# Scan of a hybrid layer stack: GpSimd works on two scan steps at a time, the residual goes to TensorE and its read-out to ScalarE

## The chip, the core and the metric

One core of a Trainium2 chip runs the whole kernel. The metric is the device time of one execution in microseconds; the kernel before took 3098.16 us (median of three runs, 3097.73 to 3105.76). Engines are called PE (TensorE), DVE (VectorE), ACT (ScalarE), POOL (GpSimd) and SP (SyncE, which here only issues DMAs).

## What is computed

Four layers over x of shape 8 x 512 x 512 (batch, position, channel): a selective state-space scan, a mixture of experts, attention, the same mixture of experts. The change touches only the first. Cut to what matters:

```python
xz = einsum('bld,kd->blk', xn, W_x)              # xn = layernorm(x)
dt = softplus(dt_raw @ W_dt.T + b_dt)
d_a = exp(dt[..., None] * a)                     # 16 states per channel
dbx = dt[..., None] * b_ssm[:, :, None, :] * xn[..., None]
h   = d_a[t] * h + dbx[t]                        # over t
y_t = einsum('bdn,bn->bd', h, c_ssm[t])
x1  = x + y + xn * D_param
```

## The kernel before

The scan works with channels on the 128 partitions and 512 positions along the row. A step k is one block of 128 channels (HC = 4 blocks c) with one group g of NG = 2 of the 16 states; STEPS = 32 steps make a batch, NSTEP = 256 steps the whole scan. Steps k and k + 1 (k even) are the two blocks of one half of the channels for the same group, so both use the same rows of B and C (`bc`, one DMA of 1 MB for every two steps, NBC = 3 buffers).

One step runs through four engines:

- POOL `feed` (line 1796) writes dt·x·B for both states into a buffer of `hb` (128x1024; HB = 5 buffers of one step).
- ACT `decay` (line 1654) writes exp(a·dt) for the two states into PSUM banks 2, 3, 4 in turn, so it can be at most one and a half steps ahead of the scan.
- DVE `scan` (lines 1292 and 1296) waits for the feed and the decays, runs two scans along the row, and multiplies the second state by C. 
- POOL `weigh_c` (line 1802) multiplies the first state by C (128x512), once its scan is done.
- PE `y_sum` (line 970) adds both states, transposed, into a PSUM bank of y, one bank for even and one for odd blocks; at g = 0 it first puts in xn·D (line 965). The feed of step k waits for the sum of step k - HB.

After the eighth group of a block, DVE `x1` (line 1302) adds the y bank onto the row buffer `xin` (which holds x), two steps behind the scan (X1_BEHIND = 2). The next sum into that bank waits for it.

Every engine executes its instructions in the order of one written plan (`scan_plan`). It is a list of items; each engine takes from it the items that it has a function for. The tables at lines 55 to 65 say at which of the 32 steps of a batch the other work stands: the preparation of the next batch (layernorm, projections, softplus with `dt_sum` on DVE at line 1283 and `dtx` on POOL at line 1787), the router of the previous batch (`route1` with line 1361, `masks` with line 1381, `pick` with lines 1389 and 1392) and its shared expert (PE lines 998, 1019, 1033, 1039; ACT line 1673; DVE lines 1315 and 1330). The feed of step k + 2 stands ahead of the scan of step k (AHEAD = 2).

```python
plan += [("scan", k), ("weigh_c", k)]
```

After the scan come a short routing chain, the experts, attention and the second mixture; they are not touched but for one small ring (OUT) that holds rows of the shared expert.

Of the kernel before, what the change touches and what calls it, by code (L numbers as in the profile page):

```python
# [15 lines left out]
P = 128  # L16
# [25 lines left out]
NG = 2  # L42
# [4 lines left out]
HB = 5  # L47
NBC = 3
AHEAD = 2
# [14 lines left out]
FIRST_DT, FIRST_SOFT = (0, 0), (("soft_exp", 3), ("soft_ln", 4), ("dt_sum", 5), ("dtx", 6))  # L64
X1_BEHIND = 2
# [20 lines left out]
ABREAST, OUT = (1, 2), (3, 4)  # L86
# [236 lines left out]
def scan_plan():  # L323
# [12 lines left out]
    for k in range(NSTEP + X1_BEHIND):  # L336
        if k + AHEAD < NSTEP:
            plan += [("feed", k + AHEAD)]
        if k < NSTEP:
            b, c, g = step_of(k)  # L340
            plan += [("scan", k), ("weigh_c", k)]
            if c % 2 == 0 and k // 2 + NBC - 1 < NSTEP // 2 and k > 0:
                plan += [("bc_in", k // 2 + NBC - 1)]
# [6 lines left out]
        if 0 < k <= NSTEP:  # L350
            plan += [("sum", k - 1)]
# [7 lines left out]
    plan += own[:OUT[0]]  # L359
    for more in chain:  # L360
# [4 lines left out]
        for kind in TAKEN_BESIDE.get(name, ()):  # L365
            plan += [i for i in pending if i[0] == kind]
            pending = [i for i in pending if i[0] != kind]
        if name == "pick4":
            plan += own[OUT[0]:]
# [204 lines left out]
class Program:  # L574
# [76 lines left out]
    def list_memory(self, sb, m):  # L651
# [3 lines left out]
        f["own"], f["twice"] = sb.cut([1]), sb.cut([1])  # L655
# [41 lines left out]
    def scan_memory(self, sb):  # L697
# [11 lines left out]
        self.hb = [sb.cut([NG, SEQ]) for _ in range(HB)]  # L709
# [187 lines left out]

    def da_bank(self, k, n):
# [12 lines left out]
def tensor_engine(p, eng):  # L911
# [44 lines left out]
    def y_sum(k):  # L956
        b, c, g = step_of(k)
        s, w, each = b % 2, p.hb[k % HB], b * HC + c
# [8 lines left out]
        for n, by in enumerate(("pool", "dve")):  # L967
            PE.wait_ge(p.weighted[by], k)
# [248 lines left out]
def vector_engine(p, eng):  # L1217
# [67 lines left out]
    def scan(k):  # L1285
        b, c, g = step_of(k)
        h = p.hb[k % HB]
        banks = [bank[p.da_bank(k, n)] for n in range(NG)]
        V.wait_ge(p.fed, k)
# [888 lines left out]
```

## Time and profile before

| | before |
|---|---|
| median of 3 runs | 3098.16 us |
| lowest, highest | 3097.73, 3105.76 us |
| profiled execution, its time | 3104.51 us |
| its span in the profile | 3102.7 us |
| busy PE, DVE, ACT, POOL | 2788.7, 1774.2, 1292.9, 1526.5 us |
| scan stage | from about 37 to 1060 us of the span |

The span is cut into 40 slices of 77.6 us on the page; slices 2 to 13 are the scan, where DVE and POOL are both at nine tenths or more. Times below are microseconds from the start of the span. "Idle before" is the time that the engine stood still just before the instruction, with what ended that wait. Groups of instructions give the total busy time and the mean of one. Durations of consecutive instructions overlap a little, so the distance from start to start is the better measure where an engine never stops.

### The profile page before, as it was taken

The page shows a single profiled execution, that of the slowest core. Times are in us where ns is not written, and L with a number is a line of the kernel's source. Part 1 is how long each engine was busy: PE and PEld are TensorE (multiplying, and loading weights), DVE is VectorE, ACT ScalarE, POOL GpSimd, SP SyncE. Part 2 cuts the span into 40 slices and gives each one's busy share as a digit, 9 for nine tenths or more (in the row PEclk, how much of TensorE's full clock was granted, in tenths as well). Part 3 has the DMA queues.
Part 4 walks back from the last instruction along what each step waited for, and adds up shares of the span by engine and source line. Part 5 has one row for each costly group of instructions (what it writes and reads, how often), then busy time and mean ns, then how long its engine had stood idle before and what let it go on. Part 6 is the DMA issues. An engine that isn't in the chain of part 4 may idle for free.

```text
span 3102.7 us, 38070 instructions
## 1 busy us (share of the span) xinstructions
PE 2788.7 (90%) x13772; PEld 1502.6 (48%) x13772; DVE 1774.2 (57%) x3723; ACT 1292.9 (42%) x2681; POOL 1526.5 (49%) x943
## 2 busy tenths in 40 slices
PE   4668989988998889988868999999899999999998
PEld 2455555655555534433335555555545454444443
DVE  5899999999999742222246666665433434222222
ACT  4557577675765401110126666767612220111111
POOL 5999999999999512211135555554300000111212
PEclk7669999999998989999989999999999999999999
DMA  5444545545545579999930000002034223999997
GB/s 183 147 165 154 192 167 165 195 164 176 174 161 179 184 259 359 347 341 337 331 107 1 28 28 28 28 29 74 28 115 171 97 85 87 307 345 345 342 353 213
DMA packets 198957, 557.80 MB, mean 180 GB/s; under 512 B 24880, under 2 KB 26800, under 8 KB 198256
## 3 DMA queue, kind: packets, MB, share of 16 engines
q1 hardware_dynamic: 180624, 513.27, 48.0%
q0 software_dynamic: 17088, 40.90, 5.8%
q8 instruction: 109, 1.79, 0.2%
q10 hardware_dynamic: 1056, 1.18, 0.1%
q14 instruction: 80, 0.66, 0.1%
HBM read 479.50 MB, written 75.79 MB: 179 GB/s over the span
## 4 chain that ended last, share of the span: by engine, by line
PE 42%; DMA 8%; DVE 4%; SPq 4%; ACT 3%; POOL 2%; issue 2%; POOLq 0%; DVEq 0%; ACTq 0%
PE bank L1099 7%; PE bank L998 5%; PE bank L1019 5%; PE bank L1146 4%; DMA arena<-in_w_up 4%; PE bank L1203 3%; PE bank L1033 3%; DMA out<-arena 3%; PE bank L1125 3%; PE bank L1180 3%; PE bank L1168 2%; SPq L2037 2%; ACT arena L1717 2%; POOL arena L1892 2%; PE bank L1192 1%
## 5 line engine op out<-in xcount | busy, mean ns | idle before, releaser
L1796 POOL TENSOR_TENSOR arena<-arena 128x1024 f32<-128x1024 f32 x256 | 605.3, 2365 | 7.1 <-PE bank L970 4.0
L1654 ACT ACTIVATE bank<-arena 128x512 f32<-128x512 f32 x512 | 346.3, 689 | 316.8 <-DVE arena L1292 198.6
L1892 POOL TENSOR_TENSOR arena<-arena 128x2048 f32<-128x2048 f32 (+3 forms) x128 | 296.6, 2320 | 285.8 <-DVE arena L1522 285.8
L970 PE MATMUL bank<-arena 128*128 128x128 f32 x2048 | 308.5, 304 | 137.8 <-POOL arena L1802 137.6
L970 PEld LDWEIGHTS bank<-arena 128*128 128x128 f32 x2048 | 262.4, 157 | 223.9 <-POOL arena L1802 176.8
L1717 ACT ACTIVATE arena<-arena 128x256 f32<-128x256 f32 (+3 forms) x512 | 285.9, 561 | 189.6 <-DVE arena L1513 159.2
L1802 POOL TENSOR_TENSOR arena<-arena 128x512 f32<-128x512 f32 x256 | 333.3, 1302 | 19.8 <-DVE arena L1292 19.8
L1099 PE MATMUL bank<-arena 128*64 128x352 f32 x2048 | 333.5, 481 | 0.0
L1292 DVE TENSOR_TENSOR_SCAN arena<-bank,arena 128x512 f32<-128x512 f32 x256 | 310.9, 1214 | 25.5 <-POOL arena L1796 19.4
L1292 DVE TENSOR_TENSOR_SCAN bank<-bank,arena 128x512 f32<-128x512 f32 x256 | 308.5, 1205 | 0.0
L1019 PE MATMUL bank<-arena 128*128 128x512 f32 x640 | 288.3, 593 | 9.1 <-ACT arena L1673 9.1
L998 PE MATMUL bank<-arena 128*128 128x512 f32 x640 | 291.3, 598 | 4.3 <-DVE arena L1330 2.4
L1033 PE MATMUL bank<-arena 128*128 128x512 f32 x640 | 286.2, 598 | 0.0
L1860 POOL DMA_INDIRECT arena<-scratch_xn,arena x64 | 68.7, 1074 | 370.1 <-DVE arena L1481 139.9
L1454 DVE TENSOR_TENSOR arena<-arena,bank 128x352 f32<-128x352 f32 x64 | 33.4, 521 | 371.0 <-PE bank L1099 325.4
L1513 DVE CUSTOM_DVE_ANT_0 arena<-bank,arena 128x256 f32<-128x256 f32 (+3 forms) x512 | 220.5, 486 | 39.6 <-PE bank L1168 34.1
L1691 ACT ACTIVATE arena<-bank 128x352 f32<-128x352 f32 x64 | 29.6, 463 | 480.2 <-PE bank L1099 423.7
L1099 PEld LDWEIGHTS bank<-arena 128*64 128x64 f32 x2048 | 146.6, 142 | 152.1 <-issue 147.5
L1019 PEld LDWEIGHTS bank<-arena 128*128 128x128 f32 x640 | 120.4, 190 | 161.6 <-issue 145.9
L1296 DVE TENSOR_TENSOR arena<-bank,arena 128x512 f32<-128x512 f32 x256 | 177.1, 692 | 18.1 <-DVE bank L1292 0.5
L1033 PEld LDWEIGHTS bank<-arena 128*128 128x128 f32 x640 | 118.9, 192 | 137.9 <-issue 137.8
L998 PEld LDWEIGHTS bank<-arena 128*128 128x128 f32 x640 | 117.6, 192 | 132.4 <-issue 126.7
(139 smaller groups left out, 4130.9 us busy)
## 6 DMA issues: line engine op xcount, KB each, us to landing
arena<-scratch_bc SPq DMA_DIRECT2D x128, 1024.0 KB, 5.4
arena<-in_w_gate SPq DMA_DIRECT2D x128, 704.0 KB
arena<-in_w_up SPq DMA_DIRECT2D x128, 704.0 KB
arena<-in_w_down SPq DMA_DIRECT2D x128, 512.0 KB
arena<-in_w_down SPq DMA_DIRECT2D x128, 192.0 KB
scratch_x<-arena SPq DMA_DIRECT2D x16, 1024.0 KB, 4.6
scratch_xn<-arena SPq DMA_DIRECT2D x15, 1024.0 KB, 4.2
arena<-scratch_x SPq DMA_DIRECT2D x44, 256.0 KB, 6.0
```

The source lines that it names most:

```text
L970: i = nc.tensor.matmul(y[:, t * P:(t + 1) * P], w[:, n, t * P:(t + 1) * P], p.ident, is_transpose=True, start=False, stop=g == GROUPS - 1 ...
L998: i = nc.tensor.matmul(out[:, :], f["swg"][:, c, j * P:(j + 1) * P], xnT[:, c, :], start=c == 0, stop=c == HC - 1)
L1019: i = nc.tensor.matmul(out[:, :], f["swu"][:, c, j * P:(j + 1) * P], xnT[:, c, :], start=c == 0, stop=c == HC - 1)
L1033: nc.tensor.matmul(out[:, :], f["shT"][:, j, t * P:(t + 1) * P], f["swd"][:, j, :], start=j == 0, stop=False)
L1099: i = nc.tensor.matmul(bank[1 + w][mine, 0:INTER], f["xeT"][k % 2][:, c, mine], f["ring"][(2 * k + half) % nw][w][:, c, :], start=c == 0, ...
L1292: nc.vector.tensor_tensor_scan(out=banks[n][:, :] if n else h[:, n, :], data0=banks[n][:, :], data1=h[:, n, :], initial=0.0, op0=ALU.mult, ...
L1513: nc.vector.tensor_tensor_reduce(out=p.sc[i % NSC][:, 0:width], in0=bank[c][:, 0:width], in1=p.amask[:, SEQ - width:], scale=-SCALE, scala ...
L1654: nc.scalar.activation(bank[p.da_bank(k, n)][:, :], block_of(p.dt, b, c), ACT.Exp, scale=p.alog[:, c, state:state + 1]).then_inc(*p.decaye ...
L1717: nc.scalar.activation(p.pr[n % 2][:, c, OFFSET[t]:OFFSET[t] + width], p.sc[i % NSC][:, 0:width], ACT.Exp, scale=-1.0, bias=p.nb[:, k % 2, ...
L1796: nc.gpsimd.tensor_tensor(out=p.hb[k % HB], in0=over(block_of(p.dtx, b, c), 1, NG), in1=p.bc[k // 2 % NBC][:, 0], op=ALU.mult).then_inc(*p ...
L1802: nc.gpsimd.tensor_tensor(out=h, in0=h, in1=p.bc[k // 2 % NBC][:, 1, 0, :], op=ALU.mult).then_inc(*p.weighted["pool"].up(k))
L1892: nc.gpsimd.tensor_tensor(out=own, in0=own, in1=over(p.rden[:, k % 2, :], 2, width), op=ALU.mult).then_inc(*p.divided.up(k))
```

## The change

- `feed` and `weigh_c` on POOL are made for two steps at once: 128x2048 and 128x1024 elements in one instruction. `hb` is now HB = 3 buffers of two steps (six steps in place of five). AHEAD = 1 counts pairs. The feed of pair n + 1 stands ahead of scan 2n; the weighing of pair n stands behind scan 2n + 1 and waits for that step's first scan.
- `sum` of both steps of a pair stands together, behind the work of the next even step.
- x is put into the y bank by PE (four 128x128 products with the identity at g = 0, per block), and `x1` becomes a plain copy from PSUM to `xin` on ACT, three steps behind.
- The waits on `fed` and on the pool's `weighted` count pairs, in `dt_out`, in the DMA of `bc` and in the sums.
- The tables of steps are new. OUT of the first mixture is 2 in place of 3, and the fetches of the last rows are spread out.

```diff
-HB = 5
+HB = 3
-AHEAD = 2
+AHEAD = 1
-PREPARE = (("x_in", 4), ("stats_a", 7), ("stats", 8), ("rstd", 8), ("apply", 11))
-TURN_S, DTR, BC, DT = (13, 13, 14, 14), 16, 15, (21, 21, 22, 25)
-SOFT = (("soft_exp", (24, 28)), ("soft_ln", (26, 29)), ("dt_sum", (27, 30)), ("dtx", (28, 31)))
-FRONT = (("stats_a", 1), ("stats", 1), ("rstd", 1), ("apply", 3), ("xn_out", 3), ("gate", 7), ("logit", 9), ("route_max", 10), ("route_exp", 12), ("route1", 13), ("masks", 15))
-TURN_F, FOLD = (5, 5, 5, 6), 18
-PICK_AT = (22, 23, 24, 27, 33, 35, 37, 41)
-GATES, UPS = (23, 26, 29, 30, 32, 35), (23, 26, 29, 30, 33, 35)
-DOWNS = (40, 41, 43, 51)
+PREPARE = (("x_in", 5), ("stats_a", 9), ("stats", 9), ("rstd", 9), ("apply", 11))
+TURN_S, DTR, BC, DT = (12, 12, 13, 13), 14, 20, (16, 17, 20, 20)
+SOFT = (("soft_exp", (20, 24)), ("soft_ln", (24, 25)), ("dt_sum", (28, 30)), ("dtx", (28, 30)))
+FRONT = (("stats_a", 2), ("stats", 2), ("rstd", 2), ("apply", 4), ("xn_out", 4), ("gate", 11), ("logit", 12), ("route_max", 14), ("route_exp", 16), ("route1", 21), ("masks", 22))
+TURN_F, FOLD = (6, 6, 7, 7), 25
+PICK_AT = (27, 30, 31, 31, 40, 42, 43, 48)
+GATES, UPS = (24, 26, 28, 30, 33, 36), (24, 27, 29, 30, 33, 36)
+DOWNS = (40, 41, 49, 54)
-X1_BEHIND = 2
+X1_BEHIND = 3
-ABREAST, OUT = (1, 2), (3, 4)
+ABREAST, OUT = (1, 2), (2, 4)
...
-        if k + AHEAD < NSTEP:
-            plan += [("feed", k + AHEAD)]
+        if k % 2 == 0 and k // 2 + AHEAD < NSTEP // 2:
+            plan += [("feed", k // 2 + AHEAD)]
-            plan += [("scan", k), ("weigh_c", k)]
+            plan += [("scan", k)] + [("weigh_c", k // 2)] * (k % 2)
...
-        if 0 < k <= NSTEP:
-            plan += [("sum", k - 1)]
+        if 0 < k <= NSTEP and k % 2 == 0:
+            plan += [("sum", k - 2), ("sum", k - 1)]
...
+            for t in range(QT):
+                nc.tensor.matmul(y[:, t * P:(t + 1) * P], p.ident, p.xin[s][:, t, c * P:(c + 1) * P],
+                                 start=False, stop=False, skip_group_check=True)
...
-    def x1(b, c):
-        x = p.xin[b % 2][:, :, c * P:(c + 1) * P]
-        V.wait_ge(p.y_summed, step_at(b, c, GROUPS - 1))
-        nc.vector.tensor_tensor(out=x, in0=x,
...
+    def x1(b, c):
+        A.wait_ge(p.y_summed, step_at(b, c, GROUPS - 1))
+        nc.scalar.copy(p.xin[b % 2][:, :, c * P:(c + 1) * P], bank[Y_BANKS[c % 2]][:, :].rearrange(
+            "p (t d) -> p t d", t=QT)).then_inc(*p.x1_added.up(b, c))
...
+    def feed(n):
+        b, c, g = step_of(2 * n)
         G.wait_ge(p.dtx_ready, b, c // 2)
+        G.wait_ge(p.bc_in[n % NBC], n)
+        if n >= HB:
+            G.wait_ge(p.y_summed, 2 * (n - HB) + 1)
+        nc.gpsimd.tensor_tensor(out=p.hb[n % HB], in0=over(half_of(p.dtx, b, c // 2), 2, NG),
+                                in1=over(p.bc[n % NBC][:, 0], 1, 2), op=ALU.mult).then_inc(*p.fed.up(n))
+
+    def weigh_c(n):
+        h = p.hb[n % HB][:, :, 0, :]
+        G.wait_ge(p.scanned, 2 * n + 1, 0)
+        nc.gpsimd.tensor_tensor(out=h, in0=h, in1=over(p.bc[n % NBC][:, 1, 0, :], 1, 2), op=ALU.mult).then_inc(
+            *p.weighted["pool"].up(n))
```

## Rows read from the trace of the kernel before

**Rows 1.** Busy time by stretch: PE, PEld, DVE, ACT, POOL, then clock, DMA share, GB/s.
```profile
480.00:620.00 140.00, 128.44 (x602) 77.79 (x600) 134.83 (x170) 95.92 (x138) 136.88 (x83) 0.98 0.54 175
620.00:760.00 140.00, 123.94 (x535) 72.46 (x533) 137.03 (x176) 90.62 (x129) 130.12 (x79) 0.94 0.52 169
```

**Rows 2.** Waits from 100 to 1150 us: who waited for whom, total, times, longest.
```profile
POOL arena L1802 <- DVE arena L1292: 19.8, 9, 2.3
POOL arena L1796 <- PE bank L970: 4.0, 3, 2.5
DVE arena L1292 <- POOL arena L1796: 6.8, 17, 0.5
DVE arena L1292 <- ACT bank L1654: 5.3, 5, 1.8
```

**Rows 3.** Timeline of a stretch with little beside the steps: start, duration, engine.
```profile
489.67 2.36 POOL L1796 TENSOR_TENSOR arena<-arena 128x1024 f32<-128x1024 f32 x1
490.42 0.97 PEld L965 LDWEIGHTS bank<-arena 128*128 128x128 f32 x8
491.99 1.28 POOL L1802 TENSOR_TENSOR arena<-arena 128x512 f32<-128x512 f32 x1
493.21 2.38 POOL L1796 TENSOR_TENSOR arena<-arena 128x1024 f32<-128x1024 f32 x1
...
496.47 1.21 DVE L1292 TENSOR_TENSOR_SCAN arena<-bank,arena 128x512 f32<-128x512 f32 x1
...
499.44 1.21 DVE L1292 TENSOR_TENSOR_SCAN arena<-bank,arena 128x512 f32<-128x512 f32 x1
```

**Rows 4.** Groups of POOL instructions by shape, whole span.
```profile
L1892 POOL TENSOR_TENSOR arena<-arena 128x2048 f32<-128x2048 f32 x32 | 115.2, 3601 | 113.9 <-DVE arena L1522 113.9
L1892 POOL TENSOR_TENSOR arena<-arena 128x1024 f32<-128x1024 f32 x32 | 60.6, 1893 | 39.1 <-DVE arena L1522 39.1
L1787 POOL TENSOR_TENSOR arena<-arena 128x1024 f32<-128x1024 f32 x16 | 37.8, 2362 | 24.3 <-DVE arena L1283 24.3
L1777 POOL TENSOR_TENSOR arena<-arena 128x4 f32<-128x4 f32 x32 | 33.2, 1038 | 2.7
```

**Rows 5.** Groups of DVE instructions by shape, 80 to 1045 us.
```profile
L1283 DVE TENSOR_TENSOR arena<-arena 128x1024 f32<-128x1024 f32 x14 | 49.5, 3538 | 0.0
L1242 DVE BATCH_NORM_STATS2 arena<-arena 128x6 f32<-128x512 f32 x52 | 32.6, 679 | 0.1
L1361 DVE TENSOR_TENSOR arena<-arena 128x256 f32<-128x256 f32 x7 | 8.8, 1252 | 0.2
L1381 DVE TENSOR_SCALAR arena<-arena 128x256 f32<-128x256 f32 x7 | 8.6, 1227 | 0.2
```

**Rows 6.** Timeline around `dt_sum` (L1283), alone at 33.60 and beside POOL.
```profile
33.60 1.22 DVE L1283 TENSOR_TENSOR arena<-arena 128x1024 f32<-128x1024 f32 x1 [20.21 <-ACT arena L1637]
...
143.41 8.67 DVE L1283 TENSOR_TENSOR arena<-arena 128x1024 f32<-128x1024 f32 x1
...
526.85 5.25 DVE L1283 TENSOR_TENSOR arena<-arena 128x1024 f32<-128x1024 f32 x1
...
533.31 1.27 POOL L1802 TENSOR_TENSOR arena<-arena 128x512 f32<-128x512 f32 x1 [2.29 <-DVE arena L1292]
...
541.69 2.13 DVE L1283 TENSOR_TENSOR arena<-arena 128x1024 f32<-128x1024 f32 x1
...
913.93 2.44 DVE L1283 TENSOR_TENSOR arena<-arena 128x1024 f32<-128x1024 f32 x1
```

**Rows 7.** Timeline at the first feeds and behind the last scan.
```profile
37.33 4.64 POOL L1796 TENSOR_TENSOR arena<-arena 128x1024 f32<-128x1024 f32 x2
...
1059.46 0.69 DVE L1302 TENSOR_TENSOR arena<-arena,bank 128x512 f32<-128x512 f32 x1 [8.00 <-PE bank L970]
```

**Rows 8.** DMA issues: size and median time to landing.
```profile
arena<-scratch_bc SPq DMA_DIRECT2D x128, 1024.0 KB, 5.4
```

**Rows 9.** One group of the page: a shared-expert product is eight matmul records.
```profile
L1019 PE MATMUL bank<-arena 128*128 128x512 f32 x640 | 288.3, 593 | 9.1 <-ACT arena L1673 9.1
```

More of the change, by code:

```diff
@@ L359, in scan_plan @@
     plan += own[:OUT[0]]
+    own = own[OUT[0]:]
     for more in chain:
@@ L365, in scan_plan @@
         for kind in TAKEN_BESIDE.get(name, ()):
-            plan += [i for i in pending if i[0] == kind]
+            taken = [i for i in pending if i[0] == kind]
             pending = [i for i in pending if i[0] != kind]
-        if name == "pick4":
-            plan += own[OUT[0]:]
+            plan += taken
+            if kind == "so":
+                plan += own[:len(taken)]
+                own = own[len(taken):]
         for _ in range(MADE_BESIDE.get(name, 0)):
@@ L654, in list_memory @@
         f["wts"], f["key"], f["row"], f["gap"] = (sb.cut([NPAIR]) for _ in range(4))
-        f["own"], f["twice"] = sb.cut([1]), sb.cut([1])
+        columns = sb.cut([2])
+        f["own"], f["twice"] = columns[:, 0:1], columns[:, 1:2]
         f["tok"] = sb.cut([CAP])
@@ L708, in scan_memory @@
         self.bc = [sb.cut([2, NG, SEQ]) for _ in range(NBC)]
-        self.hb = [sb.cut([NG, SEQ]) for _ in range(HB)]
+        self.hb = [sb.cut([2, NG, SEQ]) for _ in range(HB)]
     def row_memory(self, sb):
@@ L896, in ring_with, with states @@
         return next(r for r in self.rings if key in r.index)
+    def states(self, k):
+        return self.hb[k // 2 % HB][:, k % 2]
     def da_bank(self, k, n):
@@ L957, in y_sum @@
         b, c, g = step_of(k)
-        s, w, each = b % 2, p.hb[k % HB], b * HC + c
+        s, w, each = b % 2, p.states(k), b * HC + c
         y = bank[Y_BANKS[c % 2]]
@@ L966, in y_sum @@
                                  start=t == 0, stop=False, skip_group_check=True)
-        for n, by in enumerate(("pool", "dve")):
-            PE.wait_ge(p.weighted[by], k)
+            if b > 0:
+                PE.wait_ge(p.x_in[s], b)
+            for t in range(QT):
+                if b == 0:
+                    PE.wait_ge(p.x_first[t], 0)
+                nc.tensor.matmul(y[:, t * P:(t + 1) * P], p.ident, p.xin[s][:, t, c * P:(c + 1) * P],
+                                 start=False, stop=False, skip_group_check=True)
+        for n, (by, made) in enumerate((("pool", k // 2), ("dve", k))):
+            PE.wait_ge(p.weighted[by], made)
             for t in range(QT):
@@ L1543, in vector_engine @@
     work = {"constants": constants, "barrier": barrier, "stats": stats, "stats_a": stats_a, "apply": apply, "decay_w": decay_w,
-            "dt_sum": dt_sum, "scan": scan, "x1": x1, "hid": hidden, "so": shared_out,
+            "dt_sum": dt_sum, "scan": scan, "hid": hidden, "so": shared_out,
             "route_max": route_max, "route1": route1, "masks": masks, "folded": folded, "pick": pick, "merge": merge, "lists": lists,
@@ L1623, in dt_out @@
         if before >= 0:
-            A.wait_ge(p.fed, (before + 1) * STEPS // 2 - 1)
+            A.wait_ge(p.fed, (before + 1) * STEPS // 4 - 1)
         nc.scalar.activation(block_of(p.dtx, b, c), out[:, :], ACT.Abs, bias=p.par[:, c, 0:1])
@@ L1743, in scalar_engine @@
             "dt_out": dt_out, "soft_exp": soft_exp, "soft_ln": soft_ln, "decay_w": decay_w, "scan": decay,
-            "logit": logit, "silu": silu, "route_exp": route_exp, "up": expert_gate, "flip": flipped, "scale": scale,
+            "x1": x1, "logit": logit, "silu": silu, "route_exp": route_exp, "up": expert_gate, "flip": flipped, "scale": scale,
             "mask": exped, "pcopy": probs_flipped, "weighed": weighed}
@@ L1788, in dtx @@
                                 op=ALU.mult).then_inc(*p.dtx_ready.up(b, h))
-    def feed(k):
-        b, c, g = step_of(k)
+    def feed(n):
+        b, c, g = step_of(2 * n)
         G.wait_ge(p.dtx_ready, b, c // 2)
-        G.wait_ge(p.bc_in[k // 2 % NBC], k // 2)
-        if k >= HB:
-            G.wait_ge(p.y_summed, k - HB)
-        nc.gpsimd.tensor_tensor(out=p.hb[k % HB], in0=over(block_of(p.dtx, b, c), 1, NG), in1=p.bc[k // 2 % NBC][:, 0],
-                                op=ALU.mult).then_inc(*p.fed.up(k))
-    def weigh_c(k):
-        h = p.hb[k % HB][:, 0, :]
-        G.wait_ge(p.scanned, k, 0)
-        nc.gpsimd.tensor_tensor(out=h, in0=h, in1=p.bc[k // 2 % NBC][:, 1, 0, :], op=ALU.mult).then_inc(
-            *p.weighted["pool"].up(k))
+        G.wait_ge(p.bc_in[n % NBC], n)
[8 more added lines that the diff above has]
+            *p.weighted["pool"].up(n))
     def route_w(m):
```

12 lines of the change are left out of this document (5 added, 7 removed).

## The prediction

> **What bounds the kernel now.** I read the page's slices first: the scan fills the first third of the span, and DVE and POOL are both full in it. By stretch, POOL is busy 136.88 of 140 us and DVE 134.83, PE 128.44 [rows 1]. No engine is plainly the bound; three are near it. So the next view is who waits for whom: from 100 to 1150 us POOL waits 19.8 us for scans, DVE 6.8 us for feeds and 5.3 us for decays, POOL 4.0 us for sums [rows 2]. DVE and POOL take turns, and what counts is the sum of work on each and how much either may run ahead.
>
> **POOL now.** Where nothing stands beside, feed starts at 489.67, weighing at 491.99, the next feed at 493.21: 2.32 + 1.22 = 3.54 us a step [rows 3], 113.3 a batch. Add two `dtx` (2.33 each, from [rows 4] less the overlap) and two `rstd` chains of short instructions, the longest 1.04 [rows 4], some 1.9 each with their gaps: 121.8. A batch really takes 128.4 us: `dt_sum` of batch 0 starts at 143.41, that of batch 6 at 913.93 [rows 6].
>
> **DVE now.** Two steps back to back are 2.97 us apart (496.47 to 499.44) [rows 3]; with gaps I take 3.0, so 96 a batch. `dt_sum` is 6.8 a batch (49.5 over about 7.3 batches), `x1` 2.8, the rest of the beside-work about 20.7; 126.3 in all. Of that, `dt_sum` alone needs 1.22 and takes 3.54 on the mean beside POOL [rows 5, 6].
>
> **What the change does to each.**
> 1. *Two steps in one POOL instruction.* The fixed part of an instruction is, by start-to-start distances, 2 x 1.22 - 2.32 = 0.12 us; by durations, the attention's rows give 1893 x 2 - 3601 = 185 ns [rows 4]. Two instructions less a pair: 0.24 to 0.37 us, and I take 0.28. A pair goes from 7.08 to 6.80 (feed 4.49, weighing 2.31), a batch from 113.3 to 108.8: 4.5 us of POOL a batch, 36 in all (31 to 47). That broadcasting over the outer dimension is free is shown: `dtx` without it takes 2362 ns [rows 4], the feed with it 2.36 to 2.38 [rows 3]. If the longer form saved nothing, the 36 is lost (bound from the other side: zero).
> 2. *x1 off DVE.* 32 times 0.69 [rows 7], less the overlap: 19.5 us of DVE. The ACT copy costs about 0.6 and waits for `y_summed`, with the decays of the following steps behind it. ACT is busy 96 of 140 us [rows 1]; by the walk below it gets to the copy about when the sums are done and has 4 us before DVE needs the next decay. Cost taken: nothing; without that air it is the PE lag, up to 3.6 us a time.
> 3. *Residual on PE.* Four products like those of line 965, whose weight loads take 0.97 us for a block [rows 3]: 31 us in all, 3.9 a batch, in the pair of g = 0. PE's need is then some 116 us of a batch of 125. It is hidden if PE runs at 2.4 GHz and a sum never lags by more than the 6.8 us until the feed that waits for it; the shared expert's worst chunk before a sum (three products of 288.3 / 80 = 3.6 us [rows 9] at steps 29 and 30) falls where `dt_sum` holds the others up anyway.
> 4. *bc DMA.* Its buffer is freed 6.8 us before its feed (7.1 before) and it lands in 5.4 [rows 8]. Hidden; margin 1.3 us.
> 5. *Less room between the engines.* Before, scan k could start from the end of its feed to 1.2 us before its weighing is due, a window of 6.1 us. Now the feed of a pair ends 2.4 us before the next feed starts, and the odd step's first scan must be done 4.5 us after that: a window of 2.5 us. Each burst of DVE beyond it idles POOL.
> 6. *The shared port.* `dt_sum` reads two SBUF operands. Alone it takes 1.22 us; at 541.69 it waited for the running POOL instruction, took 2.13, and stretched the next weighing to 2.25; at 526.85 it was passed over by further POOL instructions until POOL itself stood still for 2.29 us; at 143.41 that cost 8.67 [rows 6]. 4 of 14 were passed over. After the change `dtx` stands right behind the same feed and waits for `dt_sum`, so nothing can pass it; it waits for the rest of one feed, which is now up to 4.5 us long. The same holds for lines 1361 and 1381 (1.25 and 1.23 us, some 0.33 when alone) [rows 5].
>
> The Trainium skill (SBUF — State Buffer, the section on its two separate sides) says that of a GpSimd operation and such a DVE one the second comer blocks until the first has finished. By that rule nobody waits for more than the rest of one POOL instruction, and the third rival below could not happen: its chance would go to the forecast. The trace agrees for 10 of 14 `dt_sum` and disagrees for 4, so that rival keeps a chance.
>
> **The walk.** I went through a batch pair by pair with these numbers: POOL feed(n+1) 4.49, then weighing(n) 2.31, not before the odd step's first scan; DVE 3.0 a step plus what the new tables put beside it (statistics 3.0 at steps 2 and 9, four rows of 0.68 [rows 5] and their aggregate; a pick 1.3; a shared-expert item 0.6); port operations at the end of the running feed. The weighing of pairs 0 to 15 ends, in a batch with picks at 8, 10, 11 and 16, at 6.8, 15.5, 22.3, 29.1, 35.9, 46.1, 53.7, 60.5, 67.6, 74.4, 81.2, 90, 96.8, 103.6, 113.9, 124.2. The two long ones at the end are `dt_sum` and `dtx`: 20.6 us for two pairs, 2.3 more than POOL's own work. A batch with picks at 27 to 31 takes 121.7, but leaves DVE 4 us late into the next. Two batches are 249.9, so 125.0 each. The walk has neither ACT nor PE in it; before, waits for those were 5.3 + 4.0 us over 7.5 batches [rows 2], so I add 1.3: 126.3.
>
> **Sum.** Batches 1 to 6: 6 x (128.4 - 126.3) = 13 us. Batch 0, paced by POOL, 4. Batch 7, without preparation, 4. The first scan waits for a feed of two steps (4.5 in place of 2.3 [rows 7]): -2. At the end x1 waits 8.00 us for PE's backlog of shared-expert work [rows 7]; in the new order the last sums stand behind less of it but the weighing is 1.1 longer: +2. Together 21, rounded to 20. The profiled execution took 3104.5, so 3084.5 on its scale; the median is 6.3 us lower: 3078.
>
> **The rivals.**
> - *All of POOL's saving arrives* (3060, chance 0.12). If DVE is never late, 36 us of POOL come through and the passed-over turns of `dt_sum` go too: 3098 - 38. For it: x1 is off DVE. Against: DVE's own sum, 96 + 19 + 2.2 + port waits of 8, is about 125 a batch.
> - *The lost room eats it* (3090 to 3107, likeliest 3097, chance 0.25). Stalls of 2 to 3 us a batch beyond the walk (a PE chunk at a lower clock: the stretch 620 to 760 has 0.94 granted [rows 1]; ACT behind a table load and the x1 copy; or the long form saving nothing) make six batches worth 126.3 + 2.5 = 128.8. For it: three engines busy 92% or more of a stretch [rows 1]. Against: the waits for ACT and PE were small before.
> - *Slower: the router's operations are passed over* (3117, chance 0.18). Line 1361 at step 21 has a weighing and the next feed queued on POOL ahead of any wait for DVE. If it is passed over by both, it waits 6.8 us in place of 1.5, scan 22 starts 4.8 later and POOL stands for as long. The same can happen to line 1381. At 4.8 us each it takes 4 of the 14 to undo the forecast's 20, and 6 of 14 make it slower by 9; 8 of 14 give 3078 + 39 = 3117. For it: 4 of 14 `dt_sum` were. Against: lines 1361 and 1381 average 1.25, so they seldom were.
>
> **How the numbers follow.** Forecast 3078 (3069 to 3088), chance 0.45. A difference under about 0.3% (9.3 us) can't be told from none. Faster 0.45 + 0.12 = 0.57, same 0.25, slower 0.18. The range reaches from the first rival, 3058, over the second to the edge of the third, 3110.
>
> **What would show it.** Feeds of 4.5 us and weighings of 2.36 us, 128 each; both start-to-start distances adding to 6.8 where nothing stands beside. `dt_sum` never above about 5.5 us. `dt_sum` starts 126 us apart from batch to batch. The waits of the weighing for the scan rise above 19.8 us in total (the lost room), to perhaps 60. DVE's waits for ACT and POOL's for PE stay under 20 us. The prediction is wrong if the feed of 2048 takes over 4.7 us, if POOL waits for PE or DMA by tens of us, or if line 1361 or 1381 takes over 5 us in most batches.

## The result, and the profile after

| | before | after |
|---|---|---|
| median, measured side by side (5 runs after) | 3102.38 us | 3118.29 us (3115.13 to 3123.92) |
| ratio after / before | | 1.0056 [1.0039, 1.0072] |
| profiled execution: its time, its span | 3104.51, 3102.7 us | 3123.92, 3122.1 us |
| first scan starts, last scan starts | 39.70, 1048.93 us | 40.87, 1070.64 us |
| experts start (DVE's first product of gate and up, line 1454, after 1462) | 1131.08 us | 1150.19 us |
| from there to the end of the span | 1971.6 us | 1971.9 us |

The change makes the kernel slower by 0.56%, some 17 us. The forecast was 3078, its range ended at 3110. The last two rows say where the time stands: the experts begin 19.1 us later, what follows takes as long as before, and the spans differ by 19.4. The whole loss is in the scan stage.

First what went as forecast, on POOL. Timeline of after, the same kind of stretch as [rows 3]:

```profile
497.06 2.36 POOL L1815 TENSOR_TENSOR arena<-arena 128x1024 f32<-128x1024 f32 x1
499.37 4.53 POOL L1809 TENSOR_TENSOR arena<-arena 128x2048 f32<-128x2048 f32 x1
503.86 2.37 POOL L1815 TENSOR_TENSOR arena<-arena 128x1024 f32<-128x1024 f32 x1
```

Weighing to feed 2.31, feed to weighing 4.49: 6.80 us for a pair, which was 7.08. Groups of POOL by shape, 40 to 1080 us:

```profile
L1809 POOL TENSOR_TENSOR arena<-arena 128x2048 f32<-128x2048 f32 x128 | 580.1, 4532 | 24.8 <-DMA arena<-scratch_bc 12.7 <-PE bank L985 11.5
L1815 POOL TENSOR_TENSOR arena<-arena 128x1024 f32<-128x1024 f32 x128 | 303.8, 2373 | 50.8 <-DVE arena L1307 48.7 <-DMA arena<-scratch_bc 2.0
```

The means of 4532 and 2373 ns are the forecast's. What is new stands behind the second bar: POOL now stands still in front of both, 24.8 and 50.8 us in all. Who waited for whom in after, 80 to 1100 us (total, times, longest), to be read against [rows 2]:

```profile
POOL arena L1815 <- DVE arena L1307: 48.7, 32, 4.2
DVE arena L1307 <- ACT bank L1662: 29.5, 30, 2.0
POOL arena L1800 <- DVE arena L1298: 16.7, 14, 1.4
DVE arena L1307 <- POOL arena L1809: 12.4, 14, 3.1
POOL arena L1809 <- PE bank L985: 11.5, 11, 2.6
POOL arena L1809 <- DMA arena<-scratch_bc: 9.2, 6, 2.8
```

POOL's wait for scans went from 19.8 to 48.7 us, DVE's for decays from 5.3 to 29.5, POOL's for sums from 4.0 to 11.5. So POOL did less and waited longer, and DVE is what it waited for. Why DVE is late is in its groups of after, 80 to 1080 us:

```profile
L1298 DVE TENSOR_TENSOR arena<-arena 128x1024 f32<-128x1024 f32 x15 | 41.5, 2766 | 0.0
L1360 DVE TENSOR_SCALAR arena<-arena 128x4 f32<-128x4 f32 x7 | 17.0, 2428 | 0.2
L1369 DVE TENSOR_TENSOR arena<-arena 128x256 f32<-128x256 f32 x7 | 12.8, 1827 | 0.2
L1389 DVE TENSOR_SCALAR arena<-arena 128x256 f32<-128x256 f32 x7 | 11.8, 1686 | 0.2
```

Lines 1369 and 1389 are 1361 and 1381 of before [rows 5]; 1360 is line 1352 of before, which negates four numbers per partition and took 3.0 us in its seven batches. In the forecast it doesn't occur. That line in before, duration min/median/max in ns:

```profile
L1352 DVE TENSOR_SCALAR arena<-arena x7: 170/342/891, 208.1 to 976.7; 128x4 f32<-128x4 f32 x7
```

and the three in after:

```profile
L1360 DVE TENSOR_SCALAR arena<-arena x7: 1669/2150/3275, 224.1 to 1010.3; 128x4 f32<-128x4 f32 x7
L1369 DVE TENSOR_TENSOR arena<-arena x7: 760/2042/2222, 247.4 to 1034.3; 128x256 f32<-128x256 f32 x7
L1389 DVE TENSOR_SCALAR arena<-arena x7: 293/2133/2326, 252.9 to 1040.5; 128x256 f32<-128x256 f32 x7
```

An operation that needs 0.17 us took 1.67 to 3.28 in each of seven batches. One of them, with the feed that ran beside it:

```profile
349.96 4.52 POOL L1809 TENSOR_TENSOR arena<-arena 128x2048 f32<-128x2048 f32 x1
351.23 3.27 DVE L1360 TENSOR_SCALAR arena<-arena 128x4 f32<-128x4 f32 x1
```

The feed ends at 354.48 and the negation at 354.50; in all seven batches the negation ends 0.03 us after the feed does. So it waits for the rest of the running POOL instruction, and that rest can now be twice as long. Where the line falls within POOL's cycle counts as well: in the runs below it takes 9.9 us with single steps and the new tables, and 16.1 us with pairs and the old ones.

DVE's account from the first scan to the last, after less before: line 1352/1360 +14.0 us (3.0 to 17.0), line 1361/1369 +4.0, line 1381/1389 +3.2, waits for decays +25.6 (5.6 to 31.2), waits for feeds +2.1 (14.5 to 16.6), `dt_sum` -9.2 (50.7 to 41.5, 15 each), `x1` -21.3 (30 of 678 ns and 0.9 of waits). That makes +18.4 of the 20.5 us by which this time rose (1009.23 to 1029.77).

The waits for decays crowd: 22.7 of the 31.2 us stand at steps 25 to 27 of a batch, where before has 4.4. ACT's timeline in after, one batch, some lines between left out:

```profile
387.76 1.28 ACT L1645 ACT_TABLE_LOAD   x1
389.06 1.06 ACT L1645 ACTIVATE arena<-arena 128x1024 f32<-128x1024 f32 x1
390.13 1.28 ACT L1640 ACT_TABLE_LOAD   x1
391.43 1.06 ACT L1640 ACTIVATE arena<-arena 128x1024 f32<-128x1024 f32 x1
392.39 1.28 ACT L1662 ACTIVATE bank<-arena 128x512 f32<-128x512 f32 x2
393.69 1.28 ACT L1645 ACT_TABLE_LOAD   x1
394.99 1.06 ACT L1645 ACTIVATE arena<-arena 128x1024 f32<-128x1024 f32 x1
396.06 1.28 ACT L1662 ACT_TABLE_LOAD   x1
397.36 1.30 ACT L1662 ACTIVATE bank<-arena 128x512 f32<-128x512 f32 x2
398.68 1.28 ACT L1686 ACT_TABLE_LOAD   x1
...
400.59 1.28 ACT L1662 ACT_TABLE_LOAD   x1
```

and DVE beside it:

```profile
393.10 1.22 DVE L1307 TENSOR_TENSOR_SCAN arena<-bank,arena 128x512 f32<-128x512 f32 x1 [0.59 <-ACT bank L1662]
...
398.15 1.22 DVE L1307 TENSOR_TENSOR_SCAN arena<-bank,arena 128x512 f32<-128x512 f32 x1 [1.99 <-ACT bank L1662]
...
402.61 1.22 DVE L1307 TENSOR_TENSOR_SCAN arena<-bank,arena 128x512 f32<-128x512 f32 x1 [0.72 <-ACT bank L1662]
```

Softplus is an exp (line 1640) and a log (1645) for each half of the channels, silu (1686) is the shared expert's, and each of these stands in another table than its neighbour. From 387.76 to 401.87 stand six loads of 1.28 us and only four decays, and so in six batches; in before no six loads in a row have fewer than six decays among them. The number of loads hardly changed (105 before, 100 after, 80 to 1050 us); the new tables of steps put the log of one half, the exp of the other and its log at steps 24, 24 and 25, with two silus right behind. The Trainium skill (ScalarE: Activation LUTs, What ACT_TABLE_LOAD costs) gives 1283 ns for the load and 1380 ns more for a drain. The load agrees; the drain isn't here, since the activation starts 1.30 us after its load did (387.76, 389.06) and the next load starts when that activation ends (389.06 + 1.06, 390.13).

### The profile page after: what moved, and what is told of

Read it like the earlier page. It is cut to its first block, busy times and chain, and to the rows that moved or that the text cites. A ratio compares the mean times of both kernels' runs of the same rounds, so it can differ in the third digit from the quotient of the medians.

```text
span 3122.1 us, 38187 instructions
## 1 busy us (share of the span) xinstructions
PE 2806.8 (90%) x14028; PEld 1533.7 (49%) x14028; DVE 1767.2 (57%) x3691; ACT 1310.1 (42%) x2715; POOL 1485.5 (48%) x687
## 4 chain that ended last, share of the span: by engine, by line
PE 46%; DMA 5%; DVE 4%; SPq 3%; ACT 3%; POOL 2%; issue 1%; POOLq 0%; DVEq 0%; ACTq 0%
PE bank L1114 8%; PE bank L1013 5%; PE bank L1034 5%; PE bank L1048 4%; PE bank L1161 4%; PE bank L1140 4%; DMA arena<-in_w_up 4%; PE bank L1218 3%; PE bank L1195 3%; PE bank L1183 2%; SPq L2050 2%; ACT arena L1730 2%; POOL arena L1905 2%; PE bank L1207 1%; DVE arena L1521 1%
## 5 line engine op out<-in xcount | busy, mean ns | idle before, releaser
L1809 POOL TENSOR_TENSOR arena<-arena 128x2048 f32<-128x2048 f32 x128 | 580.1, 4532 | 24.8 <-DMA arena<-scratch_bc 12.7
L985 PE MATMUL bank<-arena 128*128 128x128 f32 x2048 | 290.3, 301 | 116.6 <-POOL arena L1815 116.0
L1307 DVE TENSOR_TENSOR_SCAN arena<-bank,arena 128x512 f32<-128x512 f32 x256 | 310.7, 1214 | 55.0 <-ACT bank L1662 31.2
L1815 POOL TENSOR_TENSOR arena<-arena 128x1024 f32<-128x1024 f32 x128 | 303.8, 2373 | 50.8 <-DVE arena L1307 48.7
L1013 PE MATMUL bank<-arena 128*128 128x512 f32 x640 | 290.6, 597 | 15.5 <-ACT arena L1686 6.5
```

Source lines behind the costliest of these rows:

```text
L985: i = nc.tensor.matmul(y[:, t * P:(t + 1) * P], w[:, n, t * P:(t + 1) * P], p.ident, is_transpose=True, start=False, stop=g == GROUPS - 1 ...
L1013: i = nc.tensor.matmul(out[:, :], f["swg"][:, c, j * P:(j + 1) * P], xnT[:, c, :], start=c == 0, stop=c == HC - 1)
L1307: nc.vector.tensor_tensor_scan(out=banks[n][:, :] if n else h[:, n, :], data0=banks[n][:, :], data1=h[:, n, :], initial=0.0, op0=ALU.mult, ...
L1809: nc.gpsimd.tensor_tensor(out=p.hb[n % HB], in0=over(half_of(p.dtx, b, c // 2), 2, NG), in1=over(p.bc[n % NBC][:, 0], 1, 2), op=ALU.mult). ...
L1815: nc.gpsimd.tensor_tensor(out=h, in0=h, in1=over(p.bc[n % NBC][:, 1, 0, :], 1, 2), op=ALU.mult).then_inc(*p.weighted["pool"].up(n))
```

## The experiments

All in pairs with the kernel before on the same chip, five rounds each. Two measures stand in the table: the ratio of the times, and the start of the experts (DVE's first product of gate and up) in the one profiled execution (before 1131.08, after 1150.19). From there to the end the 17 profiles took between 1969.4 and 1980.4 us without an order that I can see, so of two profiles a difference under some 8 us in the whole says little; the ratios decide.

| kernel | ratio [95%] | experts start |
|---|---|---|
| after | 1.0056 [1.0039, 1.0072] | 1150.2 |
| move_only | 1.0025 [1.0011, 1.0040] | 1128.8 |
| move_three_behind | 1.0012 [0.9998, 1.0026] | 1126.5 |
| single_steps_new_tables | 1.0124 [1.0101, 1.0148] | 1162.4 |
| pairs_old_tables | 1.0123 [1.0095, 1.0152] | 1167.0 |
| pairs_x1_on_dve | 1.0066 [1.0045, 1.0087] | 1154.3 |
| split_pairs | 1.0146 [1.0129, 1.0164] | 1177.9 |
| more_room | 1.0072 [1.0056, 1.0087] | 1156.8 |
| same_tables_no_room | 1.0068 [1.0055, 1.0080] | 1151.0 |
| no_table_loads | 0.9991 [0.9980, 1.0002] | 1131.0 |
| room_and_no_table_loads | 1.0039 [1.0025, 1.0054] | 1135.8 |
| router_off_port | 0.9983 [0.9967, 1.0000] | 1129.3 |
| router_off_port_soft_joined | 0.9973 [0.9958, 0.9988] | 1118.3 |
| both_causes_removed | 0.9963 [0.9948, 0.9979] | 1120.0 |
| before_no_table_loads | 1.0001 [0.9986, 1.0016] | 1126.5 |
| before_router_off_port | 0.9994 [0.9981, 1.0007] | 1124.0 |

### The parts one by one

**move_only**: the kernel before with the residual on PE and x1 as a copy on ACT, two steps behind.

```diff
 # y_sum, g == 0
+            for t in range(QT):
+                nc.tensor.matmul(y[:, t * P:(t + 1) * P], p.ident, p.xin[s][:, t, c * P:(c + 1) * P],
+                                 start=False, stop=False, skip_group_check=True)
...
-        nc.vector.tensor_tensor(out=x, in0=x, in1=..., op=ALU.add)
+        nc.scalar.copy(p.xin[b % 2][:, :, c * P:(c + 1) * P], ...)
```

> The kernel before with one part of the change alone: the residual goes into the y bank on PE and x1 becomes a copy on ACT, two steps behind the scan; one step per POOL instruction and the tables of before. Theory 1 (the lost room between POOL and DVE is what made the changed kernel slower, the move itself is good): DVE is rid of 32 x 0.62 us = 19.5 us and the time falls by 5 to 15 us against before, to about 3092. Theory 2 (the move is the cost: the copy holds up the decays on ACT, the residual makes sums late on PE): 5 us or more above before, and DVE's wait for decays rises from 5 us towards 29 us. Theory 3 (the new tables are the cost): as theory 1.

**single_steps_new_tables**: the same with the new tables of steps (those of the first batch, FIRST_DT and FIRST_SOFT, with them) and x1 three behind.

```diff
-PREPARE, ..., DOWNS of before;  X1_BEHIND = 2
+PREPARE, ..., DOWNS of after;   X1_BEHIND = 3
```

> All of the change but the pairing: one step per POOL instruction, five single buffers, two steps ahead and the sums step by step as before, with the residual on PE, the copy on ACT and the new tables. Against the changed kernel this adds 128 x 0.28 = 36 us of POOL work and gives the room back. Theory 1 (room): about as fast as before or faster, 3085 to 3105. Theory 2 (the move): about the changed kernel's time, 3118. Theory 3 (the tables, with ACT's softplus and silu work crowded at steps 20 to 28): 3115 or above, since the crowding stays and POOL is slower by 36 us.

**pairs_old_tables**: after, with the tables of before (FIRST_DT and FIRST_SOFT with them).

```diff
-PREPARE, ..., DOWNS of after
+PREPARE, ..., DOWNS of before
```

> The changed kernel with the tables of steps of the kernel before (where the work beside stands); pairs on POOL, residual on PE, copy on ACT three steps behind stay. Theory 1 (room): within 10 us of the changed kernel or slower, since the tables of before are laid out for single steps. Theory 3 (tables): clearly under 3118, 3100 or less, with DVE's wait for decays back near 5 us.

**pairs_x1_on_dve**: after, with x1 back on DVE and without the residual on PE (the reverse of the first diff).

> The changed kernel with x1 back on DVE as an addition, three steps behind, and no residual on PE: pairs and new tables stay. Theory 1 (room): DVE has 19.5 us more and the room stays small, so 5 to 20 us above the changed kernel, about 3130. Theory 2 (the move is the cost): 10 us or more under the changed kernel, with DVE's wait for decays and POOL's for sums well below 29 and 11.5 us.

Measured: 1.0025, 1.0124, 1.0123, 1.0066, that is 8, 38, 38 and 20 us above before, where after is 17 above. None of the three theories comes through: move_only fits the second, single_steps_new_tables the third, pairs_old_tables speaks against the third, and pairs_x1_on_dve, 3 us above after, fits none. What follows is read from the traces.

The move alone doesn't bring the 15 to 20 us that DVE gives up. Waits of move_only, 80 to 1100 us:

```profile
ACT arena L1659 <- PE bank L977: 76.9, 26, 11.3
DVE arena L1299 <- ACT bank L1654: 22.0, 17, 1.9
```

The copy stands in ACT's order ahead of the next decays and waits for the sums 26 times, 77 us in all; DVE's waits for decays go from 5.3 to 22.0, which uses up most of the 20 us of `x1`. In the changed kernel the move gives nothing that can be told from none: 1.0056 with it, 1.0066 without, both intervals 0.003 to 0.004 wide.

The tables belong to the pairs. With the old ones the pairs lose 21 us more (1.0123): the comparison (line 1389) takes 3791 ns on the mean and `dt_sum` 4110, and POOL waits 82.6 us for scans. With the new ones single steps lose 35 us more than with the old (1.0124 against 1.0012 of move_three_behind, below); min/median/max of the router's normalising line there:

```profile
L1361 DVE TENSOR_TENSOR arena<-arena x6: 5011/7549/7672, 246.7 to 911.2; 128x256 f32<-128x256 f32 x6
```

The seventh, in the last batch, took 1.10. A median of 7.5 us for a thing of 0.42 is more than the rest of any one POOL instruction there (2.36 on the mean, 3.34 at most): POOL's next ones went first.

**move_three_behind**: move_only with the copy one step later.

```diff
-X1_BEHIND = 2
+X1_BEHIND = 3
```

> move_only with the copy on ACT three steps behind the scan in place of two. In move_only ACT waited 76.9 us at the copy for the sums, with the decays behind it, and DVE 22 us for decays. If that in-order wait is what took back the 20 us of DVE: ACT's wait at the copy falls under 25, DVE's for decays under 12, the time by 8 to 15 us, to about 3097. If the residual on PE is the cost: no change from 3109.

Measured 1.0012. The copy's waits fall from 76.9 to 16.8 us and DVE's for decays from 22.0 to 9.2, as expected; the time falls by 4 us where 8 to 15 were expected, and each of the two ratios is uncertain by as much. So the waits behind the copy are real, and their price isn't told apart from none. The rest of the move's cost stays open. One lead is that `dt_sum` takes 55.5 and 56.6 us in the two runs where it took 50.7 (15 each). But in both profiles the experts start a little before those of the kernel before, and move_only's first mixture (to the attention's first reciprocal) then takes 489.6 us where it took 484.1, with nothing in the change to explain it.

### What a longer POOL instruction is worth

**split_pairs**: after, each paired operation as two of half the size, the order and the signals as they are.

```diff
+        for i in range(2):
+            x = nc.gpsimd.tensor_tensor(out=p.hb[n % HB][:, i], in0=over(half_of(p.dtx, b, c // 2)[:, i, :], 1, NG),
+                                        in1=p.bc[n % NBC][:, 0], op=ALU.mult)
+        x.then_inc(*p.fed.up(n))
...
```

The weighing is split in the same way.

> The changed kernel with each paired POOL operation issued as two of half the size, back to back, in the same order and with the same signals: only the merging is undone. It costs POOL 0.24 to 0.37 us a pair, 31 to 47 us in all. If POOL's own work sets the pace: 3118 + 30 to 45 = about 3155. If DVE sets it (port waits, late decays): under 15 us more; shorter POOL instructions also shorten each port wait, which can bring it back to 3118 or below.

Measured 1.0146, 28 us slower than after. Groups of DVE in it, 80 to 1080 us, and its wait for feeds, 80 to 1100 us:

```profile
L1298 DVE TENSOR_TENSOR arena<-arena 128x1024 f32<-128x1024 f32 x15 | 31.0, 2070 | 0.0
L1369 DVE TENSOR_TENSOR arena<-arena 128x256 f32<-128x256 f32 x7 | 30.6, 4374 | 0.2
L1360 DVE TENSOR_SCALAR arena<-arena 128x4 f32<-128x4 f32 x7 | 10.9, 1556 | 0.2
...
DVE arena L1307 <- POOL arena L1810: 38.9, 35, 3.4
```

At the port DVE neither wins nor loses: line 1369 rises from 12.8 to 30.6 us (up to 8.1 us for one), line 1360 falls from 17.0 to 10.9, `dt_sum` from 41.5 to 31.0, line 1389 from 11.8 to 10.5, together 83.1 and 83.0. What rises is DVE's wait for feeds, from 12.4 to 38.9 us. POOL is busy 44 us more from the first scan to the last, and 28 of them are paid, near the 30 that I had set for POOL's own work. So the merging is worth 28 us in the changed kernel, and neither POOL nor DVE has time to spare: in this kernel a delay on either is mostly paid.

Long instructions make each wait at the port longer and make it rarer that a DVE operation is passed over. I count an operation as passed over when a whole POOL instruction ran within its recorded time. Of the 36 of `dt_sum` and the three router lines from the first scan to the last these are 0 in after and 4 in split_pairs, 5 in before and 8 in single_steps_new_tables. Pairs don't rule it out: one `dt_sum` each in pairs_old_tables, more_room and room_and_no_table_loads took 8.6, 9.5 and 9.9 us.

### The rival: lost room

**more_room**: after, with four buffers of two steps, four of `bc`, two pairs ahead. Room for it comes from one transposed input of the shared expert in place of two, and two halves of dt in place of three, so the second half's softplus moves to steps 32 to 40 (FIRST_SOFT and MADE_BESIDE are fitted to it).

```diff
-HB = 3
+HB = 4
-NBC = 3
+NBC = 4
-AHEAD = 1
+AHEAD = 2
-TURN_S, DTR, BC, DT = (12, 12, 13, 13), 14, 20, (16, 17, 20, 20)
-SOFT = (("soft_exp", (20, 24)), ("soft_ln", (24, 25)), ("dt_sum", (28, 30)), ("dtx", (28, 30)))
+TURN_S, DTR, BC, DT = (12, 12, 13, 13), 14, 20, (16, 17, 32, 33)
+SOFT = (("soft_exp", (20, 36)), ("soft_ln", (21, 37)), ("dt_sum", (26, 40)), ("dtx", (26, 40)))
```

> The changed kernel with room given back in pairs: four buffers of hb and of bc, and the feed two pairs ahead. The memory comes from one buffer in place of two for the turned rows of the router and two halves in place of three for dt and dtx, for which the second half's softplus moves to steps 32 to 40. Theory 1 (room): POOL's waits for scans and for dt_sum (61 us in the changed kernel) fall under 20 and its waits for the bc DMA (11 us) to nothing; 25 to 35 us under the changed kernel, about 3085 to 3095. Rival 2 (DVE's own sum is the bound: port waits of the router's operations, and decays late on ACT): under 10 us gained, since what DVE loses to the port and to ACT comes back as DVE work, not as room.

**same_tables_no_room** is its control: the same tables and sharing, but HB, NBC and AHEAD as in after.

> The control for more_room: its tables and its smaller rings, but three buffers of hb and bc and the feed one pair ahead, as in the changed kernel. All theories: within 8 us of the changed kernel (3118); what it differs by is the moved softplus, not the room.

Measured 1.0072 and 1.0068. Waits of more_room:

```profile
POOL arena L1815 <- DVE arena L1307: 52.0, 33, 5.3
DVE arena L1307 <- ACT bank L1662: 37.6, 33, 2.6
POOL arena L1809 <- PE bank L985: 17.9, 12, 2.8
...
POOL arena L1809 <- DMA arena<-scratch_bc: 2.0, 2, 1.8
```

and of its control:

```profile
POOL arena L1816 <- DVE arena L1308: 44.0, 28, 4.2
DVE arena L1308 <- ACT bank L1663: 26.9, 26, 2.0
POOL arena L1810 <- PE bank L986: 16.4, 12, 2.7
```

With a pair more of room no scan waits for a feed, which cost 10.3 us in the control, and the DMA of `bc` is in time, and nothing is gained: POOL waits for scans all the same. So with these tables the theory falls. What stands against it is DVE's sum, its waits at the port and for ACT counted in: with more room its waits for decays rise from 26.9 to 37.6 us and `dt_sum` from 43.0 to 49.2. What room is worth with the tables of after this pair can't say.

### The two causes on DVE

**router_off_port**: after, with the router's operations in forms that I expected not to wait for POOL.

```diff
-nc.vector.tensor_reduce(out=f["less"], ..., op=ALU.max)
-nc.vector.tensor_scalar(f["less"], f["less"], -1.0, None, ALU.mult)
+nc.vector.tensor_reduce(out=f["less"], ..., op=ALU.max, negate=True)
-nc.vector.tensor_tensor(out=own, in0=own, in1=over(f["inv"], 2, E), op=ALU.mult)
+for t in range(QT):
+    nc.vector.tensor_scalar(score[:, t, 0:E], score[:, t, 0:E], f["inv"][:, t:t + 1], 0.0, ALU.mult,
+                            ALU.add, accum_out=f["top"][:, t, 7:8])
-nc.vector.tensor_scalar(f["mask"][s], marked[:, :, 0:E], -2.0, None, ALU.is_equal)
+nc.vector.tensor_scalar(f["mask"][s], marked[:, :, 0:E], -2.0, 0.0, ALU.is_equal, ALU.add,
+                        accum_out=f["top"][:, 0, 7:8])
```

> The changed kernel with the three router operations of DVE that wait for POOL in other forms: the maximum is negated by the reduction itself, and the normalising and the comparison are written as scalar operations that also give a sum. In the changed kernel they take 41.6 us in seven batches (20.4 before), alone some 7. Port theory (DVE's own sum is the bound, and longer POOL instructions made these waits longer): they fall to 12 us or less and the time by 15 to 25 us, to about 3098. Late-decay theory alone: under 6 us, since DVE would use the time to wait for ACT.

**before_router_off_port**: the same three edits on the kernel before.

> The kernel before with the same new forms of the three router operations as in router_off_port. There they take 20.4 us in seven batches, so at most some 10 us can go. If the longer POOL instructions are what made them cost 21 us more, this gains 0 to 8 us (3095 to 3102), clearly less than the 18 us of the changed kernel. If it gains 18 here too, the port wait is no part of the difference between the kernels.

Measured 0.9983 and 0.9994. Against after's 1.0056 the edit is worth 0.0073 (give or take 0.0023), 23 us, within the 15 to 25 expected; on the kernel before 0.0006, 2 us, which can't be told from none (its profile has the experts 7 us earlier and the rest 7 us longer). Its lines, min/median/max in ns:

```profile
L1368 DVE TENSOR_SCALAR_CACHE_REDUCE arena<-arena x28: 274/276/281, 246.4 to 1014.4; 128x64 f32<-128x64 f32 x28
...
L1389 DVE TENSOR_SCALAR_CACHE_REDUCE arena<-arena x7: 420/420/421, 252.0 to 1019.4; 128x256 f32<-128x256 f32 x7
```

Beside a full POOL the spread is 1 to 7 ns, and what took 41.6 us in seven batches takes 13.6, the reads of the accumulators included. The Trainium skill (SBUF — State Buffer, Who interferes with whom) says that a scalar operation of DVE can contend with GpSimd, but not the form that also writes out its accumulator, and that a reduction never does. This trace agrees; the reduction takes 408 to 420 ns in it. And POOL's wait for scans falls from 48.7 to 14.9 us: it had been waiting for DVE's port waits.

**no_table_loads**: after, with the log of softplus and the silu of the shared expert beside the scan replaced by a maximum with zero, so no table is loaded there.

```diff
-nc.scalar.activation(soft, soft, ACT.Ln, bias=1.0)
+nc.scalar.activation(soft, soft, ACT.Relu, bias=0.0)
-                             ACT.Silu)
+                             ACT.Relu if m == 0 and q < BATCH - 1 else ACT.Silu)
```

> The changed kernel with ACT's logarithm of the softplus and the silu of the shared expert beside the scan computed as a maximum with zero (this leaves out both functions), so that ACT loads no function tables beside the decays: some 90 loads of 1.28 us less. If decays late on ACT cost the time (28.5 us of DVE waits), those waits go to under 5 and the time falls by 15 to 25 us, to about 3098. If the room alone is the cost, under 8 us.

**before_no_table_loads**: the same edit on the kernel before.

> The kernel before with the same functions left out as in no_table_loads (logarithm of the softplus and silu of the shared expert beside the scan, both a maximum with zero). Late-decay theory: before, DVE waited 5 us for decays, so this gains 0 to 6 us where the changed kernel gained 17. Rival (table loads cost the same in any order of steps and so explain nothing of the difference): 12 us or more.

**room_and_no_table_loads**: more_room with this edit.

> more_room with the functions left out: neither room nor table loads are short. DVE-sum theory: DVE waits for nobody (under 5 us for ACT, under 3 for POOL), the port waits of dt_sum and the router stay at about 90 us, and the time is 3129 less 25 to 35, about 3098. If it comes to 3080 or less, room was short after all, hidden behind the late decays.

Measured 0.9991, 1.0001, 1.0039. In the changed kernel the loads cost 20 us (0.0065, give or take 0.0020), in the kernel before nothing that can be told from none. With more room the late softplus has a new wait: DVE still waits 29.4 us for decays, now 14 times with up to 4.9 us, ACT's copy of x1 waits 31.8 us for sums. So room didn't combine with the cure as I had expected; the tables of more_room cost too much of their own to say what room alone would be worth.

**both_causes_removed**: router_off_port and no_table_loads together.

> The changed kernel with the router operations off the port and with the logarithm of the softplus and the silu beside the scan left out (a maximum with zero). Apart these gained 18 and 17 us. If they are two separate terms of DVE's sum: 30 us or more under the changed kernel, 3080 to 3090, 12 us or more under before. If they overlap (the same idle time counted twice): about 3098.

Measured 0.9963: 29 us below after, where the two gains alone add up to 43, and 11 below before. That is just short of the 30 and 12 that I had set for two separate terms. By the intervals the missing 14 us are uncertain by some 10, so they overlap in part. One group of DVE, 80 to 1080 us, and the waits, 80 to 1100 us:

```profile
L1298 DVE TENSOR_TENSOR arena<-arena 128x1024 f32<-128x1024 f32 x15 | 57.0, 3803 | 0.0
...
DVE arena L1307 <- POOL arena L1809: 26.2, 34, 3.1
...
POOL arena L1809 <- PE bank L985: 21.0, 21, 3.2
...
POOL arena L1809 <- DMA arena<-scratch_bc: 13.2, 6, 3.5
...
POOL arena L1815 <- DVE arena L1307: 9.1, 5, 2.1
```

POOL waits for scans 9.1 us in place of 48.7 and DVE is now the one that waits, for feeds, while POOL waits for sums and for the DMA of `bc`. The terms that were hidden behind DVE come out here. And `dt_sum`, which neither edit touches, takes 57.0 us in place of 41.5: no one takes over 4.8 us, but they meet more of the running feed. These 15.5 us at the port are as much as what is missing; that they are the reason is my reading, and no run tests it. What is left of the change with both causes away is 11 us, half of the 20 forecast.

**router_off_port_soft_joined**: a remedy for each cause that keeps the full computation. The exp of the second half comes a step earlier and both logs stand at step 24.

```diff
-SOFT = (("soft_exp", (20, 24)), ("soft_ln", (24, 25)), ...)
+SOFT = (("soft_exp", (20, 23)), ("soft_ln", (24, 24)), ...)
```

> As router_off_port, and both logarithms of the softplus stand together at step 24 (exponentials at 20 and 23), which saves one pair of table loads a batch and empties step 25. Both causes together: another 3 to 10 us less, about 3090, with DVE's wait for decays at 15 us or less. If late decays don't count: as router_off_port.

Measured 0.9973 [0.9958, 0.9988], 26 us below after and 8 us below before. DVE's waits for decays are 10.1 us, line 1645 loads its table 7 times in place of 14 and line 1640 never. This version beats both kernels. Over router_off_port it gains 3 us, which can't be told from none.

## Why the prediction was wrong

**POOL's instructions (step 1): right.** 4532 and 2373 ns, 6.80 us a pair. The longer form saves what it was to save, and undoing it alone costs 28 us (split_pairs); POOL's own work is busy 125.1 of 140 us where it was 133.5 (means of the two stretches of [rows 1]).

**The walk: the place of the failure.** `dt_sum` of batch 0 and of batch 6 in after:

```profile
148.57 3.71 DVE L1298 TENSOR_TENSOR arena<-arena 128x1024 f32<-128x1024 f32 x1
...
936.18 1.22 DVE L1298 TENSOR_TENSOR arena<-arena 128x1024 f32<-128x1024 f32 x1
```

787.61 / 6 = 131.3 us a batch, where the walk gave 125.0 and the forecast 126.3; before it was 128.4. In six batches that is 30 of the 40 us between the 21 forecast and the 19 lost. Batches 0 and 7, for which the sum has 4 us of gain each, together lost 3.5 (the scans outside these six batches took 238.7 us and take 242.2); that they fail by the same terms isn't shown. Two terms of the walk fail.

- *Step 6, the port.* It named `dt_sum` and lines 1361 and 1381 (which take 0.43 and 0.29 us alone, for the 0.33 given), and missed line 1352, since in the trace of before it is a short thing (0.43 us on the mean). It cost 14 us more, and the three together 21. A short operation's own duration says nothing of what it can wait: that is set by the instruction it meets. For `dt_sum` the step was right: at most 4.34 us, and 41.5 us for 15 in place of 50.7.
- *Step 2, "cost taken: nothing".* I took ACT's spare time from the mean busy share (96 of 140 us) and looked at the x1 copy alone. The tables that the change lays anew put six table loads among four decays. DVE's waits for decays rose by 25.6 us to 31.2, 3.9 a batch, against my sign of under 20 in all; I had 1.3 us a batch for ACT and PE together. The copy as such has its cost where it stands two behind (move_only).

Taking the mean 2.43 us of line 1360 and 29.5 / 7.5 = 3.9 us for decays onto the walk's 125.0 gives 131.3. Such waits overlap, so the sum is no proof by itself. The proof is in the runs: 23 us for the three router lines, 20 for the table loads, 29 for both, and 2 and none on the kernel before.

**Step 3, PE: half right.** POOL's waits for sums rose from 4.0 to 11.5 us, more than hidden, less than a bound. Once DVE is quicker they are 21 (both_causes_removed).

**Step 4, the bc DMA: wrong in size.** Its margin of 1.3 us was of a median landing. POOL's feeds wait 9.2 us for it, up to 2.8 at a time; landings in after have a median of 5.5 us, but reach 9.5 once the scan runs. Hidden in after behind DVE: more_room took the wait away and gained nothing.

**Start and end.** Right. The first scan starts 1.2 us later (forecast 2). From the last scan to the experts it took 82.2 us and takes 79.6: the tail gained 2.6 (forecast 2). The scale was less good: the profiled execution was 6.3 us above the median of three runs, but 2.1 above that of the five measured side by side, by which the forecast would read 3082.

**The rivals.** *The lost room* had the direction of the waits (POOL's for scans rose to 48.7, my mark was 60), but room taken back gains nothing where it was tried. *The router passed over* gave 3117, near the measured 3118, by a mechanism that didn't happen in the changed kernel: line 1369 never took more than 2.22 us and 1389 not more than 2.33. It does happen in the neighbours (7.67 us with single steps, 8.1 in split_pairs), and once in seven in before (4.13 us at line 1361). The right time by the wrong mechanism is not a hit. What I should have priced is the ordinary wait for the rest of a feed at three lines a batch, and not the rare one. By the rule of the Trainium skill that stands in the prediction nobody waits longer than that. The trace of after agrees; those two kernels and the three long `dt_sum` of other kernels with pairs don't.

**What stays open**: why the move alone costs 4 to 8 us by the ratio, what room alone is worth with the tables of after, and what decides whether POOL's next instruction passes a waiting DVE operation. Not tried apart were the sums put together by pairs, the smaller OUT ring and the spread fetches.

## What to carry to other kernels

When two engines share a port, doubling one's instructions can double what every small operation of the other waits: list all that can meet it, the shortest too, and take them off the port (a reduction that negates, a form that writes its accumulator) before merging. Lay a schedule out by the worst half dozen steps of each engine, its table loads counted in, not by its busy share. And an instruction moved to an engine that works in order brings its wait along: put it late enough that what it waits for is long done.

## What the runs showed of the hardware

- A 128x4 scalar operation on DVE, 0.17 us alone, took 2.15 us in the median and 3.28 at most beside POOL operations of 4.5 us, and ended 0.03 us after the running one in 7 of 7 cases; the accumulating form of a 128x64 one took 274 to 281 ns in 28 of 28 cases beside the same POOL.
- POOL's `tensor_tensor` took 4532 ns for 128x2048 and 2373 for 128x1024 (means of 128): two short ones less a long one are 0.21 us.
- A DVE operation was passed over by queued POOL instructions more often when these were short: 8 of 36 with single steps and 0 with pairs under the same tables, 4 with the pairs split. The longest took 9.9 us, an operation of 1.22 us alone, and that with pairs.
- A table load took 1283 ns each time (130 in after), started when the activation before it had ended, and the next activation started 0.01 us after it.
